# A two-layer graph network on one core: step words packed for TensorE's registers, and rows by source in four parts in place of three

## What is computed

```python
h = jnp.maximum(_layernorm(x, axis=-1), 0.0)
msg = h[src] @ W_msg.T + b_msg + edge_embed[jnp.clip(edge_type, 0, 8)]
messages = jax.ops.segment_sum(msg, dst, num_segments=12500)
x = x + _gru_cell(messages, h, W_ih, W_hh, b_ih, b_hh)
h = jnp.maximum(_layernorm(x, axis=-1), 0.0)
agg = jax.ops.segment_sum(h[dst], src, num_segments=12500)
g = ((1.0 + eps) * h + agg) @ W1.T + b1
g = (g - jnp.mean(g, axis=0)) * jax.lax.rsqrt(var + 1e-5) * gamma + beta
x = x + jnp.maximum(g, 0.0) @ W2.T + b2
```

## The kernel before

| pairs | beside the picks |
|---|---|
| 0 to 32 | nothing (own rows in pairs 0 to 24) |
| 32 to 48 | 4 chunks a pair, 63 in all |
| 48 to 55 | 6 chunks a pair, 39 in all |
| after | tail, 23 chunks |

## Time and profile before

### The profile page before, as it was taken

One profiled execution on the slowest core, in us unless ns is written; L12 is line 12 of the kernel. 1 busy time (PEld: TensorE's weight loads), 2 busy tenths in 40 slices (PEclk: granted clock), 3 DMA queues, 4 the chain that ended last, 5 costly groups with the idle time before them and its releaser, 6 DMA issues.

```text
span 5648.7 us, 78171 instructions
## 1 busy us (share of the span) xinstructions
PE 3221.0 (57%) x17495; PEld 2607.6 (46%) x17496; DVE 2670.9 (47%) x4799; ACT 1608.2 (28%) x3266; POOL 3336.2 (59%) x3510
## 2 busy tenths in 40 slices
PE   4566666666666665665943333333335666666767
PEld 3344444444444444444733222322324565556656
DVE  7566665666665656664641011111003444445557
ACT  4323222222222322222432222222222222221137
POOL 0666666666666666665136666666666666655563
PEclk8555555555555555555975555555556888878889
DMA  4222222222222111111222222222223444445455
GB/s 144 79 69 67 68 66 68 67 67 67 69 68 66 54 44 43 44 44 39 65 74 74 71 71 74 74 71 74 70 71 128 159 161 146 154 152 174 175 186 181
DMA packets 311629, 514.05 MB, mean 91 GB/s; under 512 B 68678, under 2 KB 227065, under 8 KB 295517
## 3 DMA queue, kind: packets, MB, share of 16 engines
q0 software_dynamic: 106944, 226.05, 13.4%
q1 hardware_dynamic: 118669, 242.40, 13.0%
q10 hardware_dynamic: 85904, 44.17, 2.6%
HBM read 331.72 MB, written 180.64 MB: 91 GB/s over the span
## 4 chain that ended last, share of the span: by engine, by line
another core or an unknown queue 33%; PE 25%; issue 20%; DVE 9%; ACT 5%; ACTq 2%; DVEq 2%; POOL 1%; DMA 1%; SPq 0%; POOLq 0%
PE ps L1700 6%; PE ps L1715 6%; PE ps L1569 4%; PE ps L1583 3%; PE ps L1591 2%; DVE sb_Y L1356 2%; ACT sb_counts L740 2%; DVE sb_blks L1157 2%; PE ps L1739 2%; ACT sb_ring L852 1%; ACTq L848 1%; PE ps L1712 1%; DVEq L1165 1%; DVE sb_oh L1146 1%
## 5 line engine op out<-in xcount | busy, mean ns | idle before, releaser
L649 POOL DMA_INDIRECT rows_by_src<-sb_ring,sb_posE x1664 | 1631.5, 980 | 966.1 <-ACT sb_ring L852 485.3
L626 POOL DMA_INDIRECT sb_ring<-msg_table,sb_stepE x1664 | 1576.9, 948 | 1034.6 <-SPq L466 498.6
L1700 PE MATMUL ps<-sb_H,sb_oh 128*128 x3520 | 725.0, 367 | 1161.9 <-issue 517.6
L1700 PEld LDWEIGHTS ps<-sb_H,sb_oh 128*128 128x128 f32 x3520 | 620.3, 263 | 1265.6 <-issue 1263.8
L1569 PE MATMUL ps<-sb_ring,sb_oh 128*128 x3520 | 926.9, 435 | 216.8 <-issue 208.4
L1569 PEld LDWEIGHTS ps<-sb_ring,sb_oh 128*128 128x128 f32 x3520 | 779.0, 319 | 310.0 <-issue 306.0
L1338 DVE TENSOR_SCALAR sb_oh<-sb_oh,sb_cf 128x512 f32<-128x512 bf16 x440 | 215.4, 503 | 1212.4 <-remote 933.9
L852 ACT COPY sb_ring<-ps 128x512 f32<-128x512 f32 x416 | 242.8, 584 | 1913.0 <-remote 1308.1
L740 ACT CAST sb_counts<-ps 54x512 bf16<-54x512 f32 x440 | 254.8, 579 | 1757.3 <-remote 1198.7
L1189 DVE TENSOR_TENSOR sb_Y<-sb_Y,ps 128x512 f32 x440 | 300.0, 682 | 636.6 <-remote 576.6
L1583 PE MATMUL ps<-sb_oh,sb_toh 128*54 128x128 bf16 x1760 | 320.0, 301 | 261.2 <-issue 252.3
(11 more groups left out here) (225 smaller groups left out, 3855.2 us busy)
## 6 DMA issues: line engine op xcount, KB each, us to landing
sb_stepE<-rows_by_src SPq DMA_DIRECT2D x114, 1088.0 KB
sb_oh<-step_targets SPq DMA_DIRECT2D x110, 512.0 KB
rows_by_src<-sb_cf ACTq DMA_DIRECT2D x294, 136.0 KB
sb_ring<-msg_table,sb_stepE POOLq DMA_INDIRECT x1664
rows_by_src<-sb_ring,sb_posE POOLq DMA_INDIRECT x1664
sb_ring<-rows_by_src SPq DMA_DIRECT2D x11, 1088.0 KB, 5.1
msg_table<-sb_oh SPq DMA_DIRECT2D x14, 448.0 KB, 3.2
sb_oh<-in_x SPq DMA_DIRECT2D x49, 128.0 KB, 2.1
```

The lines of the kernel that those rows point to most:

```text
L626: pool.indirect_dma_start(out=ring[:, m % RGROUPS * G + q, 0:F], out_offset=None, in_=table_d[:, :], in_offset=bass.IndirectOffsetOnAxis(a ...
L649: pool.indirect_dma_start(out=rows_d[:, :], out_offset=bass.IndirectOffsetOnAxis(ap=posE[:, m * G + q:m * G + q + 1], axis=0), in_=ring[:, ...
L1700: m = mm(picked_ps[:, ds(slot, P)], pick[g][:, q * P:(q + 1) * P], H[:, ds(off, P)], start=False, stop=True, skip_group_check=True)
```

## The change

- **Packed words.** `slotrow` and `needrow` are gone. A table `wordrow` has one int32 for a step, with the batch's number in the high bits and the block's offset in the low ones (relative to the group's first in layer 0, in full in the picks). PE loads 16 words once for a chunk into one of two sets of registers, in group 1 of the chunk before (`load_words`), and takes slot, offset and the count of `wait_tiles` out of them by shifts and masks. DVE makes both tables in the setup (`step_words`), from one more transpose by PE.
- **Pick one-hots.** DVE makes the one-hot of a group two groups earlier in its program (`PICKS_AHEAD`).
- **Own rows in a loop.** SP copies H's two blocks of a chunk to a fixed buffer (`own_in`), PE transposes from there, and PE's pick loop is no longer unrolled.
- **Parts.** `PASSES` is 640, 640, 256, 128 and `SUM_RATE` 4, 6, 8. The plan is then: picks alone in pairs 0 to 25 and 37 to 44, 4 chunks a pair in pairs 25 to 37 (47 chunks), 6 in pairs 44 to 52 (47), 8 in pairs 52 to 55 (23), and a tail of 15. The pads of 98 more pairs of part and block are stored by ACT in layer 0 (392 in place of 294).

The core of the diff, without the setup's tables (their layout in `rowtab` and the sizes of temporaries follow from it):

```diff
-PASSES = (896, 512, 256)
-SUM_RATE = (4, 6)
+PASSES = (640, 640, 256, 128)
+SUM_RATE = (4, 6, 8)
+PICKS_AHEAD = 2
...
 # DVE, setup
+            def step_words():
+                dve.wait_ge(S("tables_kept"), 1)
+                off = tables_i[T_BLOCK:T_BLOCK + SB, :]
+                first = off.rearrange("s (g q) -> s g q", q=G)[:, :, 0:1].to_broadcast([SB, P // G, G])
+                vs.tensor_tensor(step_rel.rearrange("s (g q) -> s g q", q=G), off.rearrange("s (g q) -> s g q", q=G), first,
+                                 ALU.subtract)
+                vs.tensor_scalar(msg_words, step_tile, 9, None, ALU.logical_shift_left)
+                link(vs.tensor_scalar(pick_words, step_tile, 14, None, ALU.logical_shift_left))
+                vs.tensor_tensor(msg_words, msg_words, step_rel, ALU.bitwise_or)
+                vs.tensor_tensor(pick_words, pick_words, off, ALU.bitwise_or).then_inc(S("words_made"), 1)
...
 # SP, picks
+            def own_in(c, k):
+                wait(sp, "h2_ps", c - 1)
+                sp.dma_start(own_buf[k], H[:, ds(c * GW, GW)]).then_inc(S(f"own_in{k}"), 16)
...
                 if not sums:
                     next_loc()
+                if own and not (isinstance(c, int) and c + 2 >= TURNS):
+                    own_in(c + 2, k)
...
 # DVE, picks
                 for p in range(GPC):
-                    layer1_pick(j, k, p)
+                    if p < GPC - PICKS_AHEAD:
+                        layer1_pick(j, k, p + PICKS_AHEAD)
+                    elif not last:
+                        layer1_pick(j + k, 1 - k, p + PICKS_AHEAD - GPC)
...
 # PE
-            def step_offsets(c, row=steprow):
-                nc.tensor.load(regs, row[0:1, ds(c * CH, CH)])
-            def step_slots(c):
-                nc.tensor.load(slots, slotrow[:, ds(c * CH, CH)])
-            def wait_tiles(name, n):
-                pe.wait_ge(S(name), pe.value_load(needrow[:, ds(n, 1)], min_val=1, max_val=TGROUPS))
+            def load_words(c, k):
+                nc.tensor.load(words[k], wordrow[:, ds(c * CH, CH)])
+            def wait_tiles(name, value):
+                pe.reg_alu(need, pe.snap(value + 1), 1, ALU.max)
+                pe.wait_ge(S(name), pe.snap(need, min_val=1, max_val=TGROUPS))
+            def msg_rel(k, s):
+                return within(word(k, s, MSG_TOP) & 511, (s % G) * P)
...
 # PE, sum_rows
-                    o = bank(1 + g)[:, 0:P] if q == 0 else ps[:, 1 + g, ds(rel(g, q), P)]
-                    tile = pe.snap(slots[s], min_val=0, max_val=(2 * CH - 1) * RW)
-                    mm(o, oh[:, k, s, :], ringf[:, ds(tile, F)], start=False, stop=True, skip_group_check=True)
+                    o = bank(1 + g)[:, 0:P] if q == 0 else ps[:, 1 + g, ds(msg_rel(k, s), P)]
+                    slot = within((word(k, s, MSG_TOP) >> 9) & (2 * CH - 1), 2 * CH - 1)
+                    mm(o, oh[:, k, s, :], ringf[:, ds(slot * RW, F)], start=False, stop=True, skip_group_check=True)
...
 # PE, layer0
-                step_offsets(c)
-                step_slots(c)
...
-                    wait_tiles("tiles_in", n)
+                    wait_tiles("tiles_in", word(k, g * G + G - 1, MSG_TOP) >> 11)
                     sum_rows(g, k, n)
+                    if g == 1 and not (isinstance(c, int) and c == CHUNKS - 1):
+                        load_words(c + 1, 1 - k)
...
 # PE, picks
-                    h2T(c, k)
-                step_offsets(c)
-                step_slots(c)
+                    h2T(j, k)
...
-                        off = pe.snap(regs[g * G + q], min_val=0, max_val=(BLOCKS - 1) * P)
-                        slot = pe.snap(slots[g * G + q], min_val=0, max_val=(CH - 1) * P)
+                        off = within(word(k, g * G + q, PICK_TOP) & ((1 << 14) - 1), (BLOCKS - 1) * P)
+                        slot = within((word(k, g * G + q, PICK_TOP) >> 14) & (CH - 1), CH - 1)
...
-            pick_loop(pe, picks_and_sums, TURNS // 2)
+            pick_loop(pe, picks_and_sums)
```

More of the change, by code:

```diff
@@ L112, in pick_phases @@
     plan.append((at, PAIRS, None, 0, 0))
-    return [p for p in plan if p[1] > p[0]]
+    plan = [p for p in plan if p[1] > p[0]]
+    assert plan[-1][1] - plan[-1][0] == 1
+    return plan
 PICK_PHASES = pick_phases()
@@ L248, in build_gnn @@
         rbuf, zbuf, tbuf, nbuf, hnbuf, cell_x = ([ob(2 * a + k) for k in range(2)] for a in range(6))
+        own_buf = [type_rows[:, k, 0:2 * GW].bitcast(f32) for k in range(2)]
         locb = [ohf[:, k * 1024:(k + 1) * 1024].bitcast(bf16) for k in range(2)]
@@ L710, in _ @@
                     act.wait_ge(S("tables_T"), 1)
-                    nc.scalar.copy(needs_i[32:32 + SB, :], bank(7)[32:32 + SB, G - 1:P:G])
+                    nc.scalar.copy(step_tile, bank(7)[0:SB, P:2 * P])
                     nc.scalar.copy(tables_i[:, :], bank(7)[0:TABR, 0:P]).then_inc(S("tables_kept"), 1)
@@ L1120, in _ @@
             dve.wait_ge(S("fields_moved"), 8)
[L1121 to L1122 removed]
+            early = 2
+            starts, firsts = fldi[1][:, 896:896 + NPASS * NBK], fld[1][:, 1300:1300 + NPASS * NBK]
             vs.tensor_copy(starts[:, 0:early * NBK], bank(7)[:, 256:256 + early * NBK])
[L1124 removed]
+            link(vs.tensor_copy(starts[:, early * NBK:], bank(3)[:, 256:256 + (NPASS - early) * NBK]))
             nc.vector.sem_inc(S("starts_read"), 1)
@@ L1214, in sum_blocks @@
             def sum_blocks():
-                tmp = digits.bitcast(bf16)[:, 0:SS * (BLOCKS - 1)].rearrange("p (s b) -> p s b", s=SS)
+                halves = [(a, min(a + SS // 2 + 1, SS)) for a in range(0, SS, SS // 2 + 1)]
                 vs.tensor_scalar(step_at, const("step"), float(P), None, ALU.mult)
@@ L1373, in picks_and_sums @@
                     sum_add(sums[-1][0], g, offs[-1])
-            dve.wait_ge(S("steprow_in"), 96)
+            dve.wait_ge(S("steprow_in"), 80)
+            for g in range(PICKS_AHEAD):
+                layer1_pick(0, 0, g)
             pick_loop(dve, picks_and_sums)
@@ L1539, in _, with word, within, rel @@
                     m.then_inc(S("src_col"), 1)
[L1541 to L1542 removed]
+            words = [[pe.alloc_register(f"step_word{k}_{q}") for q in range(CH)] for k in range(2)]
             sum_regs = [pe.alloc_register(f"sum_off{q}") for q in range(CH)]
[L1545 to L1555 removed]
+            need = pe.alloc_register("step_need")
+            def load_words(c, k):
+                nc.tensor.load(words[k], wordrow[:, ds(c * CH, CH)])
+            def word(k, s, top):
+                return pe.snap(words[k][s], min_val=0, max_val=top)
+            def within(value, top):
+                return nc.s_assert_within(pe.snap(value), 0, top, skip_runtime_bounds_check_because="a field of a step's word")
+            MSG_TOP, PICK_TOP = (TILES << 9) - 1, (TILES << 14) - 1
+            def wait_tiles(name, value):
[3 more added lines that the diff above has]
+                return within(word(k, s, MSG_TOP) & 511, (s % G) * P)
+            def rel(g, q, regs=sum_regs):
                 first = pe.snap(regs[g * G], min_val=0, max_val=(BLOCKS - 1) * P)
```

97 lines of the change are left out of this document (55 added, 42 removed).

## The result

The changed kernel takes 6205.67 us (median of 3 runs, 6191.15 to 6229.80) against 5654.18: 1.0985 times the time before, 95% interval 1.0928 to 1.1042. It is slower by about 10%, where about 3% faster was forecast with a range up to 5750. The profiled execution has a span of 6227.9 us.

A forecast was written before the change was run, and what follows sets the result against it. It took PE as the bound in layer 0 and the picks, through its own program and late semaphore increments. The terms summed to -173 us from the profiled 5650.5, giving 5480 as median, about 3% faster, range 5300 to 5750.

The forecast's parts named there:

- Layer 0, -127: Packed words in layer 0: fewer loads on PE save 2.3 us in each of 55 pairs, -127 us (0 to -457).
- Rival 2: No gain in layer 0 or picks alone, since POOL and late increments set their pace: 5640 us, chance 0.20.
- Picks alone, -32: Packed words in the 32 pairs of picks without sums: 1 us less each, -32 us (0 to -192).
- Unpacking in the pairs with sums, +52: Unpacking beside pick matmuls, less saved loads: 2.6 us more in each of 20 pairs, +52 us (-69 to +170).
- rival 1: PE's sequencer becomes the bound at 0.65 us per matmul; pairs with sums pay 7.4 us each: 5755 us, chance 0.17.
- One-hots ahead, -93: Picks with sums: half of PE's wait for DVE's one-hots goes, -93 us (0 to -186).
- Parts, +59 - 40 + 5: Four parts: denser sums lengthen the picks by 59 us, the tail loses 40, one more part's start costs 5.
- Setup, +3: Tables made in the setup, with one transpose and SP's longer chain: +3 us (0 to 8).
- Own rows, 0: PE's rolled pick loop and SP's copy: 5 to 15 us of back edges hidden beside POOL's work, 0.
- Rival 4, +100: Own rows' copy waits for late increments of PE's transposes, exposed 4 us in 25 pairs: +100, 5580 us, chance 0.07.

The follow-up runs named there:

- the dose of five: Kernel before plus five plain register instructions ahead of three of every four row and pick matmuls: 6438.90 for 5580.84 us (slow chip), 5293.99 for 4792.62 (quick).
- the kernel without the words: Parts, one-hots ahead and own rows in a loop together on the kernel before, PE loading registers as before: 5615.83 for 5580.84 us, 1.0056, slow chip.
- the dose of two: Kernel before plus two plain register instructions ahead of three of every four matmuls: 4926.16 for 4792.62 us, 1.0281, on a quick chip only.

## Why the prediction was wrong

The sum, term by term. **Layer 0, -127:** it grew by 342 on the first chip, and by 285 from the words alone on the chip of 5581. This is the term that failed, and it holds the error of reasoning: "in layer 0 it stands against 0.435 us of array time per matmul, so little shows". On a quick chip nothing shows, but for another reason: POOL's floor of 2081 us covers the 181 us by which PE's busy time grew. On the chip of the prediction layer 0 stood 457 us above that floor, so it covered nothing, and there a register instruction may be held for 0.7 us; array time doesn't hide 1004 such. The prediction priced an instruction by its median and left out the maxima in the very same rows: 726 ns at L1557 and 725 at L1569, for kinds with medians of 159 and 42. It also saw increments arrive up to 14 us late and took this for an outer disturbance that "an edit of PE's program can't remove". That may be so for the increments. The held-up instructions, however, grow with what PE executes, from 131 to 1004.

What late increments and held-up instructions have in common is shown, though not what they are. On both quick chips neither is there: no register instruction on PE over 0.5 us but the loads, and no "remote" in the lists of waits. On all slow ones both are, and a count over the raw records of the changed kernel (plain and fused instructions, the whole run) puts the held-up instructions where POOL's indirect DMAs are: up to 3 us after the start of one, 1720 of 18907 take over 0.5 us (9%), 3 to 5 us after it 18 of 2970, later than that none of 1393, and after the last indirect DMA none of 335. A row from the tail:

```profile
L1609 PEldq FUSED_REGOPS  x180: 137/159/165, 6085.8 to 6164.4; - x180
```

Between 137 and 165 ns, all 180. The same count for the kernel before on a quick chip has none of 10426 within 3 us, so POOL's DMAs alone don't do it. This is a coincidence in time; a kernel without POOL's DMAs was not run. Two other explanations don't fit the profiles. Fetching more instructions: the queues of kind "instruction" carried 84 and 50 packets with the dose of five on either kind of chip. Slower DMAs: the packets of POOL's queue took 13.4% of 5649 us before on a slow chip and 16.1% of 4792 on a quick one, 757 and 772 us.

**The other half of that term, the gain:** the loads and waits that the words remove were given 11 us of PE time per pair and 2.3 of pace. Halving the waits without unpacking gave 14 us in layer 0, and moving the loads 19 (against the kernel without the words). The idle time of 0.78 us before a group was real and no bound. Rival 2 was nearly right in this.

**Picks alone, -32:** on the first chip the 32 pairs took 1568.6 us (1228.8 for pairs 0 to 25, 339.8 for 37 to 44), where the first 32 pairs had taken 1386.4: +182. Pairs 0 to 24 alone took 48.8 us each, where they had 42.6 (1172.0 for 1023.5 us). On the chip of 5581 the words alone are 157 of it, and on a quick chip 3, so this loss goes with the kind of chip as layer 0's does.

**Unpacking in the pairs with sums, +52:** this depends on the chip too, and the other way. On a quick chip it is (756.7 - 640.4)/16 = 7.3 us per pair with four chunks, for 2.6 forecast; rival 1 had said 7.4. The doses say why: a plain instruction whose record is 0.032 us costs 0.10 to 0.12 us of pace. The prediction had put in 0.1 us for each of the five, which was right, but let the matmul's own 0.325 us run beside them in full, though the sequencer had already been busy in that time. Part of the 7.3 is the clock, 0.84 for 0.88. On the slow chip of 5581, however, the 20 pairs with four and six chunks got 6 us shorter and not 52 longer; the three with eight grew by 14. Why the same unpacking costs nothing in the 20 is open; the granted clock was higher with the words (0.84 for 0.78), and the loads that they remove can be held up as well, but no run separates this. On the first chip the pairs with four chunks took 51.7 us (620.7/12), for 47.7 forecast, those with six 56.7 (453.5/8) for 56.0, and those with eight 62.7 (188.2/3) for 63: the one-hots' gain of 4.6, 3.2 and 4 us did not come, and the words cost less there than forecast, so that the sixes and eights are close by luck.

**One-hots ahead, -93:** 0 on both kinds of chip. "These are late next" was the right sentence with the wrong weight: on the slow chip not half but all of PE's wait turned up as DVE's.

**Parts, +59 - 40 + 5:** right on a quick chip, where the picks grew by 60 and the tail fell by 40; on a slow one they weren't timed alone. After the change the tail is 40 us shorter (162 for 202 from the last pick to the end). **Setup, +3:** 0. **Own rows, 0:** +10 on a quick chip. The Trainium skill ("Runtime: NRT & Kernel Launch", Instruction fetch mechanics) says that a taken branch breaks the sequential prefetch. The number fits the 5 to 15 us that the back edges' rows would have made, but the run doesn't separate the branches from the copy on SP. Rival 4, +100, did not come in.

Of the rivals the first named the right engine and the right sign, but priced it too low: 5755, just outside the range, for 6206. It counted 0 in layer 0 and the picks alone and gave no loss there, where the loss was. The range failed for the same reason: the words' term in these stages had 0 as its upper bound.

**What stays open:** what holds PE's instructions back on some chips and not on others, and whether late increments and held-up instructions are one thing; and why 880 instructions fewer gain almost nothing where 6600 more cost some 480 us. With more instructions "remote" waits shrink (ACT's copy in the picks from 1308 us to 121) while waits that end with PE's own matmuls grow (529 to 1941). That would suit one backlog that PE's slack absorbs at first; no run shows it. The words alone have no run on a slow chip; their 456 us there are the difference of two kernels that share the other three parts.

## What to carry to other kernels

Price an instruction on an engine's sequencer by the pace that it takes, from start to start, and by the longest of its records, not by their median: here 0.032 us in the rows, 0.10 to 0.12 in the pace, and often 0.7 on the slow chips while POOL's indirect DMAs ran. Packing several numbers into a register saves loads and pays for each use with instructions in the inner loop; with a use per matmul, that trade lost here on both kinds of chip. A wait that is taken from one engine is no gain if it turns up on the next, as with the one-hots. And a time should be compared only with the kernel before on the same chip.

## What the runs showed of the hardware

The same program takes 4791 to 4793 us on two chips and 5579 to 5654 on the others (16 to 18% more), with a similar granted clock (0.653 and 0.646). Nearly all of it lies in the two stages with POOL's indirect DMAs: 2080 for 2537 us in layer 0 and 2156 for 2538 in the picks, while the cell and norms take 199 us on both. Where PE isn't held up, 1664 gathers at 1.25 us are the whole of layer 0, and 9757 (the dose of two) to 13118 register instructions (the words) on PE fit under them for nothing. Two plain register instructions behind each other start 0.093 us apart though each record is 0.032 us long.
